# Maxima rows sent between two parts of a packing, and two lone heads scored large, large, small, small

## The chip, the cores and the metric

The kernel runs on one core of a Trainium2 chip. The metric is the time of one execution on the device in microseconds (us); three executions of the kernel before gave 2126.93, 2128.16 and 2131.79, median 2128.16. All profile rows come from one profiled execution of 2130.74 us. Engines: PE is TensorE's matmul, PEld its weight load, DVE is VectorE, ACT is ScalarE, POOL is GpSimd, and SP is SyncE, which here only issues DMAs.

## The reference

Two layers. Layer 0 takes x of shape (2, 2048, 256), normalises it, and runs a differential attention; layer 1 is a small attention over 256 features and a second small attention over its 16 picked heads. The change touches layer 0's attention alone:

```python
q = qkv[..., :2 * Hx].reshape(Bx, 2 * NQ, Sx, HD)        # 32 query heads of 16 features
k = qkv[..., 2 * Hx:2 * Hx + G].reshape(Bx, NKV, Sx, HD) # 8 key heads
scores = jnp.einsum('bhqd,bhkd->bhqk', q, k) / math.sqrt(HD)
scores = jnp.where(causal, scores, -jnp.inf)             # 2048 x 2048, causal
aw = jax.nn.softmax(scores, axis=-1)
aw = aw[:, :, 0] - lam * aw[:, :, 1]
attn = jnp.einsum('bhqk,bhkd->bhqd', aw, v) * (1.0 - LAMBDA_INIT)
```

## The kernel before

Layer 0's attention is done in 16 **groups** (2 batches by 8 key heads); a group has 4 query heads that share one key head. float32 numbers are split into bf16 parts (`part[0]`, `part[1]`, `part[2]`) whose products are added up, so that the PE can multiply in bf16. A product of queries and keys is therefore two matmuls into one bank of PSUM: a **large** one with 64 rows of contraction (four pairs of parts) and a **small** one with 34 rows (two more pairs, and two rows that subtract the query's maximum). The even heads of a group lie in partitions 0 to 63, the odd ones in 64 to 127, so the matmuls of an even and of an odd head use different rows of the PE.

Each group goes over its scores twice. In pass A, 80 **units** find each query's largest score: `unit_head` (L908) makes 128 queries by up to 512 keys for each of two heads, and DVE reduces it (L643, L640). In pass B, 36 **steps** make the softmax: in a step each head's scores of 128 keys by 512 queries are made (`score`, L938), ACT takes the exponential (L771), and the PE multiplies by V two steps later (`meet_v`, L980). Units run ahead of the steps: 46 units of a group are done before its first step, and a table (`PLACES`) says at which places of a step the next units stand. `two_heads(n, hp, u)` scores the two heads of pair `hp` with the unit `u` threaded between them; where the table gives no unit, `u` is None and the two heads stand alone. That is so at six places of each group (step 0 pair 1; steps 2, 3, 10, 20 and 35 pair 0), and in the last group, whose units run out at step 15, at 45 places: 6 x 15 + 45 = 135 in all. At steps 0, 3 and 10 such a matmul has 512 columns, at 2, 20 and 35 it has 256.

The B pass of block j (512 queries; blocks 0 to 3 begin at steps 0, 3, 10 and 21) needs the block's maxima in two rows of `q_pack`. They go from DVE over POOL and the PE to ACT, which copies them to `m_rows` (`take_maxima`, L746); then SP sends them with four small DMAs (`maxima_rows`, L386). The PE waits for these at the block's first step, and the waiting instruction is the large matmul of head 0.

SP also fills the packs of the next group: `pack` issues 36 DMAs of 64 KB (`pack_part`, L314 for keys, L316 for queries; 18 of part 0, 12 of part 1 and 6 of part 2) and one for V (L379). It begins when the last step of the group before is through, which frees the buffers. SP works through its program in order: in iteration g it does the pack of group g + 1, then the maxima rows of block 2 of group g, then the next group's rows to DRAM and back (L351 to L367), then the rows of block 3, and those of blocks 0 and 1 of group g + 1. The PE needs the new pack at the first unit of group g + 1, which stands in step 15.

Of the kernel before, what the change touches and what calls it, by code (L numbers as in the profile page):

```python
# [23 lines left out]
C = 512  # L24
# [18 lines left out]
STEPS = len(B_STEPS)  # L43
# [5 lines left out]
UNITS = len(A_UNITS)  # L49
# [20 lines left out]
def masked(u):  # L70

    return u in MASKED


def width_a(u):
    j, t, c, _ = A_UNITS[u]
    return P * (t + 1) if c == j else C
# [113 lines left out]
def layer0_attention(nc, sems, keep, early, x, Wqkv, lq1, lk1, lq2, lk2, c0, wmod0, c1, wmod1):  # L191
# [3 lines left out]
    with ExitStack() as ctx:  # L195
# [102 lines left out]
        def regions(buf):  # L298

            n = ROWS * 2 * D  # L300
            return scratch[buf][0:n], scratch[buf][n:n + ROWS * P], scratch[buf][n + ROWS * P:]
# [5 lines left out]
        def pack_part(queue, buf, p, sides):  # L307

            for n2 in range(2):
                for r, (pq, pk) in enumerate(zip(PARTS_Q[n2], PARTS_K[n2])):  # L310
                    for side in sides:
                        at = HALF * side + HD * r
                        if pk == p:
                            queue.dma_start(k_pack[buf][at:at + HD, n2, :], part[p][HD * QH:HD * (QH + 1), :]).then_inc(packs_in, 16)  # L314
                        for h in range(side, QH if pq == p else 0, 2):
                            queue.dma_start(q_pack[buf][at:at + HD, h // 2, n2, :], part[p][HD * h:HD * (h + 1), :]).then_inc(packs_in, 16)  # L316
# [5 lines left out]
        @block.sync  # L322
        def _(sp):
            for layer, c in enumerate((c0, c1)):
                for n in range(B):
                    sp.dma_start(cT[:, layer, :, n], c[n, :].rearrange("(k p) -> p k", p=P),
                                 allow_slow_non_contiguous=True).then_inc(cT_in, 16)

            def load_x(n, unused):

                if unused is not None:
                    sp.wait_ge(xhat_ready, upto(unused))
                sp.dma_start(xg[:, :, :], x_rows[bass.ds(upto(n * ROWS), ROWS), :].rearrange("(r p) d -> p r d", p=P)) \
                    .then_inc(x_loaded, 16)

            load_x(0, None)
            sp.dma_start(wmods[:, 0, :, 0:2 * D], wmod0.rearrange("(k p) n -> p k n", p=P)[:, :, 0:2 * D]).then_inc(wmod_a_in, 16)
            sp.dma_start(wqkv[:, :, :], Wqkv.rearrange("(k p) n -> p k n", p=P)).then_inc(wqkv_in, 16)
            load_x(1, 1)
            sp.dma_start(wmods[:, 0, :, 2 * D:6 * D], wmod0.rearrange("(k p) n -> p k n", p=P)[:, :, 2 * D:6 * D]).then_inc(wmod_b_in, 16)  # L340
            sp.dma_start(wmods[:, 1, :, :], wmod1.rearrange("(k p) n -> p k n", p=P)).then_inc(wmod_b_in, 16)
            for k, v in enumerate((lq1, lk1, lq2, lk2)):
                sp.dma_start(lam_in[:, k, :], v.rearrange("(o n) -> o n", o=1).broadcast_to([P, P])).then_inc(lam_inputs, 16)

            def rows_to_dram(n, buf):

                sp.wait_ge(rows_ready, WPARTS * (n + 1))
                q, k, v = regions(buf)  # L350
                sp.dma_start(q.rearrange("(c p r) -> p c r", c=4, p=P), qkvT[:, 0:4, :]).then_inc(rows_out, 16)  # L351
                sp.dma_start(k.rearrange("(p r) -> p r", p=P), qkvT[:, 4, :]).then_inc(rows_out, 16)
                sp.dma_start(v.rearrange("(r p e) -> p r e", r=2, p=P), qkvT[:, 5, :].rearrange("p (r e) -> p r e", r=2)) \
                    .then_inc(rows_out, 16)

            def heads_from_dram(n, buf):


                sp.wait_ge(rows_out, 48 * (n + 1))
                if n:  # L360
                    sp.wait_ge(parts_ready, n)
                q, k, _ = regions(buf)
                by_head = q.rearrange("(b e h r) -> e b h r", b=BLOCKS, e=HD, h=QH)
                for h in range(QH):
                    sp.dma_start(headT[HD * h:HD * (h + 1), :].rearrange("e (b r) -> e b r", b=BLOCKS), by_head[:, :, h, :]) \
                        .then_inc(heads_in, 16)
                sp.dma_start(headT[HD * QH:HD * (QH + 1), :].rearrange("e (a b r) -> e a b r", a=QH, b=BLOCKS // QH),  # L367
                             k.rearrange("(b e a r) -> e a b r", b=BLOCKS // QH, e=HD, a=QH)).then_inc(heads_in, 16)

            def pack(n, buf, steps_done):  # L370

                if steps_done is not None:
                    sp.wait_ge(pv_done, upto(START + steps_done))
                    sp.wait_ge(parts_ready, upto(n + 1))
                for p in range(3):
                    if steps_done is None:
                        sp.wait_ge(*part_made(p))
                    pack_part(sp, buf, p, range(2) if steps_done is not None else (0,))
                sp.dma_start(v_tile[buf][:, :, 0:HD], regions(buf)[2].rearrange("(t p d) -> p t d", p=P, d=HD)).then_inc(v_in[buf], 16)  # L379

            def maxima_rows(count, buf, j):

                sp.wait_ge(m_copied, upto(count))
                for h in range(QH):
                    at = HALF * (h % 2) + SMALL
                    sp.dma_start(q_pack[buf][at:at + 2, h // 2, 1, C * j:C * (j + 1)], m_rows[2 * TB * h:2 * TB * (h + 1), :]) \  # L386
                        .then_inc(m_rows_in, 16)

            rows_to_dram(0, 0)
            heads_from_dram(0, 0)  # L390
            rows_to_dram(1, 1)
            sp.wait_ge(pool_consts, POOL_CONSTS)
            pack(0, 0, None)
            heads_from_dram(1, 1)
            maxima_rows(1, 0, 0)
            maxima_rows(2, 0, 1)

            for g in range(GROUPS):
                par, more = g % 2, g + 2 < GROUPS
                if g == GROUPS - 1:  # L400
                    sp.wait_ge(rows_ready, WPARTS * GROUPS)
                    sp.wait_ge(rows_out, 48 * GROUPS)
                    load_weights(sp)
                if more:
                    load_x(g + 2, g + 2)
                if g + 1 < GROUPS:
                    pack(g + 1, 1 - par, STEPS * g)
                maxima_rows(4 * g + 3, par, 2)
                if more:
                    rows_to_dram(g + 2, par)  # L410
                    heads_from_dram(g + 2, par)
                maxima_rows(4 * g + 4, par, 3)
                if g + 1 < GROUPS:
                    maxima_rows(4 * g + 5, 1 - par, 0)
                    maxima_rows(4 * g + 6, 1 - par, 1)
# [397 lines left out]
        def _(pe):  # L813
# [85 lines left out]
            def unit_head(u, n):  # L899

                j, t, c, hp = A_UNITS[u % UNITS]
                buf, side = u // UNITS % 2, SIDES[n]
                w, q = width_a(u % UNITS), C * j + P * t
                at = 2 * u + n
                rows = slice(HALF * side, HALF * (side + 1))
                if at >= A_RING:
                    pe.wait_ge(a_maxed, at - A_RING + 1)
                ins = pe.matmul(a_bank[at % A_RING][:, 0:w], q_pack[buf][rows, hp, 0, q:q + P], k_pack[buf][rows, 0, C * c:C * c + w],  # L908
                                start=True, stop=not masked(u % UNITS))
                if not masked(u % UNITS):  # L910
                    ins.then_inc(a_scored, 1)
# [32 lines left out]
            def two_heads(n, hp, u):  # L944


                short = u is not None and width_a(u % UNITS) < C
                score(n, 2 * hp, 0)
                if u is not None:
                    unit_head(u, 0)  # L950
                if short:
                    mask_head(u, 0, 0)
                    mask_head(u, 0, 1)
                score(n, 2 * hp, 1)
                if u is not None and not short:
                    mask_head(u, 0, 0)
                    mask_head(u, 0, 1)
                score(n, 2 * hp + 1, 0)
                if u is not None:
                    unit_head(u, 1)  # L960
                score(n, 2 * hp + 1, 1)
                if u is not None:
                    mask_head(u, 1, 0)
                    mask_head(u, 1, 1)

            def meet_v(n):

# [41 lines left out]
            for n in range(TAIL):  # L1009
                g, s = n // STEPS, n % STEPS  # L1010
# [858 lines left out]
```

## Time and profile before

| what | value |
|---|---|
| executions | 2126.93, 2128.16, 2131.79 us |
| profiled execution, its span | 2130.74 us, 2129.2 us |
| PE busy | 2016.2 us (95%) |
| DVE busy | 1731.2 us (81%) |
| ACT busy | 1499.7 us (70%) |
| POOL busy | 689.2 us (32%) |

The span runs from the first to the last instruction; 1.5 us of the execution lie around it. Groups of layer 0 begin at about 103.8 us and repeat every 104 us or so until 1752; layer 1 and what lies between follow. A waits row gives who waited for whom: us in total, times, the longest. A timeline row gives start and length in us, engine, line, operation, tiles, the shape of the first instruction, how many were joined, and in brackets the idle time before the first and what ended it. Instructions of one line are joined even where their shapes differ. A windows row gives a stretch, its length, each engine's busy time and count, the granted clock as a share of 2.4 GHz, and the DMA engines' share and rate.

### The profile page before, as it was taken

Reading aid. Unit: us, or ns where it says so; the run is one execution under the profiler, and the core shown is the slowest. Engines: PE = TensorE matmul, PEld = TensorE weight load, DVE = VectorE, ACT = ScalarE, POOL = GpSimd, SP = SyncE. Lnnn points to the kernel's source line nnn. Section 1 sums busy time; section 2 is a strip of 40 time slices with the busy share of each in tenths; the row PEclk is TensorE's granted clock in tenths of the full one; section 3 lists DMA queues with packets and bytes.
Section 4 is the critical chain, followed back from the end, with each engine's and each line's share of the span. In section 5 each row is a group of like instructions: output and inputs, shape, how many; then the busy total and the mean of one; then the engine's idle time right before and its main releaser. Section 6 shows DMA issues by size and latency. Waiting matters only on the chain. (4 is left out here: it accounts for less than half of the span.)

```text
span 2129.2 us, 43957 instructions
## 1 busy us (share of the span) xinstructions
PE 2016.2 (95%) x16204; PEld 904.0 (42%) x16204; DVE 1731.2 (81%) x3986; ACT 1499.7 (70%) x3065; POOL 689.2 (32%) x1246
## 2 busy tenths in 40 slices
PE   7899999999999999999999999999989999979895
PEld 6243433343334343434333333333333328746674
DVE  3989898989898989898989898888889927833788
ACT  2178787878787878887878878787868782423664
POOL 2214141414232333323232324242411213410678
PEclk8599999999999999999999999999999999989998
DMA  7230403031313122222212121313120003110111
GB/s 179 32 61 8 74 14 69 19 64 24 59 27 55 33 49 39 44 45 38 47 35 49 34 51 31 54 29 54 29 48 23 12 1 99 40 50 1 31 50 50
DMA packets 138423, 93.10 MB, mean 44 GB/s; under 512 B 90977, under 2 KB 127969, under 8 KB 138209
## 3 DMA queue, kind: packets, MB, share of 16 engines
q1 hardware_dynamic: 137632, 89.12, 20.4%
q8 instruction: 128, 2.10, 0.4%
q10 hardware_dynamic: 576, 1.18, 0.3%
q14 instruction: 87, 0.70, 0.1%
HBM read 31.00 MB, written 20.97 MB: 24 GB/s over the span
## 5 line engine op out<-in xcount | busy, mean ns | idle before, releaser
L771 ACT ACTIVATE probs<-b_bank 128x512 f32<-128x512 f32 (+1 forms) x2304 | 1156.6, 579 | 261.8 <-PE b_bank L938 255.0
L643 DVE TENSOR_REDUCE m_part<-a_bank 128x1 f32<-128x512 f32 (+3 forms) x2016 | 1168.8, 636 | 158.5 <-PE a_bank L908 115.7
L938 PE MATMUL b_bank<-q_pack,k_pack 34*128 34x512 bf16 (+7 forms) x5120 | 869.9, 347 | 17.6 <-DMA q_pack<-m_rows 17.6
L908 PE MATMUL a_bank<-k_pack,q_pack 64*128 64x512 bf16 (+3 forms) x2560 | 811.5, 357 | 19.4 <-DVE m_part L643 14.1
L980 PE MATMUL acc<-probs,v_tile 128*32 128x512 f32 (+3 forms) x5120 | 588.3, 541 | 3.1 <-POOL probs L508 0.8
L938 PEld LDWEIGHTS b_bank<-q_pack,k_pack 34*128 34x128 bf16 (+1 forms) x5120 | 309.1, 94 | 456.4 <-ACT probs L771 327.2
L908 PEld LDWEIGHTS a_bank<-k_pack,q_pack 64*128 64x128 bf16 x2560 | 237.4, 94 | 322.7 <-DVE m_part L643 204.9
L508 POOL TENSOR_SCALAR_AFFINE_SELECT probs<-probs 128x512 f32<-128x512 f32 (+1 forms) x192 | 151.7, 790 | 643.3 <-ACT probs L771 643.2
L640 DVE CUSTOM_DVE_ANT_0 a_bank<-a_bank,mask_a 128x384 f32<-128x384 f32 (+3 forms) x544 | 251.6, 513 | 33.3 <-PE a_bank L908 31.8
L980 PEld LDWEIGHTS acc<-probs,v_tile 128*32 128x32 f32 x5120 | 108.1, 108 | 161.3 <-issue 96.7
L523 POOL TENSOR_TENSOR o_w<-o_rl,signs 128x16 f32<-128x16 f32 x64 | 14.4, 226 | 418.7 <-DVE o_rl L666 418.7
L918 PE MATMUL a_bank<-future,pick 64*128 64x128 bf16 x960 | 128.3, 218 | 0.0
L475 POOL TENSOR_TENSOR rest<-headT,part 80x256 f32<-80x256 f32 x120 | 98.1, 818 | 0.0
L918 PEld LDWEIGHTS a_bank<-future,pick 64*128 64x128 bf16 x960 | 83.4, 95 | 22.7 <-issue 1.0
L740 ACT ACTIVATE part<-headT 80x256 bf16<-80x256 f32 x128 | 82.0, 651 | 2.7 <-DMA headT<-scratch 2.7
L480 POOL TENSOR_TENSOR part<-rest,part 80x256 bf16<-80x256 f32 x120 | 80.0, 667 | 9.6
L844 PE MATMUL b_bank<-hT,wqkv 128*128 128x256 f32 x280 | 79.7, 407 | 0.0
L640 DVE DVE_READ_ACCUMULATOR2_ANT m_part<- 128x1 f32 x544 | 76.8, 141 | 0.0
L732 ACT ACTIVATE qkvT<-b_bank 128x256 f32<-128x256 f32 x84 | 32.2, 383 | 58.4 <-PE b_bank L844 44.6
L1499 PE MATMUL score_banks<-qkT 128*128 128x512 f32 (+3 forms) x160 | 66.2, 546 | 0.9 <-DVE attn L1572 0.9
L844 PEld LDWEIGHTS b_bank<-hT,wqkv 128*128 128x128 f32 x280 | 47.8, 190 | 30.2 <-ACT probs L771 19.7
L490 POOL TENSOR_TENSOR m_neg<-zeros,m_max 128x16 bf16<-128x16 f32 x64 | 14.1, 221 | 139.4 <-DVE m_max L650 139.4
(206 smaller groups left out, 1722.0 us busy)
## 6 DMA issues: line engine op xcount, KB each, us to landing
q_pack<-part SPq DMA_DIRECT2D x372, 64.0 KB, 2.4
k_pack<-part SPq DMA_DIRECT2D x186, 64.0 KB, 2.3
headT<-scratch SPq DMA_DIRECT2D x80, 128.0 KB, 3.9
scratch<-qkvT SPq DMA_DIRECT2D x16, 512.0 KB, 2.9
xg<-in_L_attn_x SPq DMA_DIRECT2D x16, 256.0 KB, 2.7
scratch<-qkvT SPq DMA_DIRECT2D x32, 128.0 KB, 2.9
q_pack<-m_rows SPq DMA_DIRECT2D x256, 2.0 KB
x<-in_L_attn_x SPq DMA_DIRECT2D x16, 256.0 KB, 6.2
```

What stands on the lines that cost most here:

```text
L475: pool.tensor_tensor(piece(rest, i, PIECES), by_position(i, PIECES), piece(part[0], i, PIECES), ALU.subtract) \
L480: ins = pool.tensor_tensor(piece(part[2], i, PIECES), piece(rest, i, PIECES), piece(part[1], i, PIECES), ALU.subtract)
L508: pool.affine_select(out=blk, in_=blk, compare_op=ALU.is_ge, fill=0.0, base=0, pattern=[[0, QH]] + [[0, blocks]] * (blocks > 1) + [[1, P]] ...
L640: dve.tensor_tensor_reduce(out=bank[:, 0:w], in0=bank[:, 0:w], in1=mask_a[:, C - w:C], scale=1.0, scalar=NEG, op0=ALU.add, op1=ALU.max, ac ...
L643: dve.tensor_reduce(out, bank[:, 0:w], AX.X, ALU.max).then_inc(a_maxed, 1)
L740: act.activation(piece(part[0], i, PIECES), by_position(i, PIECES), ACT.Copy).then_inc(part0_ready, 1)
L771: act.activation(probs[:, n % P_RING, h, at:C], b_bank[bank_no(("B", n, h))][:, at:C], ACT.Exp, scale=HD ** -0.5) \
L844: ins = pe.matmul(bank[:, 0:D], wqkv[:, k, P * w:P * (w + 1)], hT[:, k, :], start=k == 0, stop=k == 1)
L908: ins = pe.matmul(a_bank[at % A_RING][:, 0:w], q_pack[buf][rows, hp, 0, q:q + P], k_pack[buf][rows, 0, C * c:C * c + w], start=True, stop= ...
L918: ins = pe.matmul(a_bank[at % A_RING][:, w - P:w], pick[rows, m, :], future[rows, m, :], start=False, stop=m == 1)
L938: ins = pe.matmul(b_bank[bank_no(slot)][:, at:at + C - q], k_pack[par][rows, n2, P * kt:P * (kt + 1)], q_pack[par][rows, h // 2, n2, C * j ...
L980: ins = pe.matmul(acc[32 * h:32 * (h + 1), q:C], v_tile[par][:, kt, :], probs[:, n % P_RING, h, at:at + C - q], start=kt == 0, stop=s == J ...
```

## The change

Two edits, which don't depend on each other. First, `pack` can take the arguments of a `maxima_rows` call and makes it after part 0's DMAs; in iteration g the rows of block 2 are sent there and no longer behind the whole pack. The last iteration, which has no pack, sends them as before. Second, `two_heads` without a unit issues large, large, small, small and no longer large, small, large, small. With a unit nothing changes.

```diff
-            def pack(n, buf, steps_done):
+            def pack(n, buf, steps_done, rows=()):
...
                     pack_part(sp, buf, p, range(2) if steps_done is not None else (0,))
+                    if p == 0 and rows:
+                        maxima_rows(*rows)
...
                 if g + 1 < GROUPS:
-                    pack(g + 1, 1 - par, STEPS * g)
-                maxima_rows(4 * g + 3, par, 2)
+                    pack(g + 1, 1 - par, STEPS * g, (4 * g + 3, par, 2))
+                else:
+                    maxima_rows(4 * g + 3, par, 2)
...
             def two_heads(n, hp, u):
-                short = u is not None and width_a(u % UNITS) < C
+                if u is None:
+                    for small in range(2):
+                        for h in range(2 * hp, 2 * hp + 2):
+                            score(n, h, small)
+                    return
+                short = width_a(u % UNITS) < C
```

SP's queue in the first iteration of the loop, kernel before. `part0` to `part2` are the parts, `q_pack0` is the pack that group 0 is being scored from, `k_pack1` and `q_pack1` are those of group 1:

```order
L314 DMA k_pack1<-part0 16x2048 x2
L314 DMA k_pack1<-part1 16x2048 x2
L316 DMA q_pack1<-part1 16x2048 x4
L314 DMA k_pack1<-part1 16x2048
L316 DMA q_pack1<-part1 16x2048 x2
L314 DMA k_pack1<-part1 16x2048
L316 DMA q_pack1<-part1 16x2048 x2
L314 DMA k_pack1<-part2 16x2048 x2
L316 DMA q_pack1<-part2 16x2048 x4
L379 DMA v_tile1<-scratch1 128x16x16
L386 DMA q_pack0<-m_rows 2x4x128 x4
L351 DMA scratch0<-qkvT 128x4x256
```

The same place in the changed kernel (its lines are numbered two or three higher):

```order
L314 DMA k_pack1<-part0 16x2048 x2
L388 DMA q_pack0<-m_rows 2x4x128 x4
L314 DMA k_pack1<-part1 16x2048 x2
L316 DMA q_pack1<-part1 16x2048 x4
L314 DMA k_pack1<-part1 16x2048
L316 DMA q_pack1<-part1 16x2048 x2
L314 DMA k_pack1<-part1 16x2048
L316 DMA q_pack1<-part1 16x2048 x2
L314 DMA k_pack1<-part2 16x2048 x2
L316 DMA q_pack1<-part2 16x2048 x4
L381 DMA v_tile1<-scratch1 128x16x16
L351 DMA scratch0<-qkvT 128x4x256
```

The four maxima DMAs have moved up past 18 pack DMAs and the one of V; nothing else on SP has moved.

The PE at step 10 of group 1, kernel before. The `b_bank` rows are pass B's scores: `b_bank1` is head 0's (large, then small), `b_bank2` head 1's; `a_bank` rows are units:

```order
L908 MATMUL a_bank2<-k_pack1,q_pack1 128x512
L908 MATMUL a_bank0<-k_pack1,q_pack1 128x512
L938 MATMUL b_bank1<-q_pack1,k_pack1 128x512 x2
L938 MATMUL b_bank2<-q_pack1,k_pack1 128x512 x2
L908 MATMUL a_bank1<-k_pack1,q_pack1 128x512
L908 MATMUL a_bank2<-k_pack1,q_pack1 128x512
```

The same place in the changed kernel:

```order
L911 MATMUL a_bank2<-k_pack1,q_pack1 128x512
L911 MATMUL a_bank0<-k_pack1,q_pack1 128x512
L941 MATMUL b_bank1<-q_pack1,k_pack1 128x512
L941 MATMUL b_bank2<-q_pack1,k_pack1 128x512
L941 MATMUL b_bank1<-q_pack1,k_pack1 128x512
L941 MATMUL b_bank2<-q_pack1,k_pack1 128x512
L911 MATMUL a_bank1<-k_pack1,q_pack1 128x512
L911 MATMUL a_bank2<-k_pack1,q_pack1 128x512
```

Head 1's large matmul, with its wait for a free bank, now stands ahead of head 0's small one.

## Rows read from the trace of the kernel before

**Rows 1.** The page's head: the span, and PE's busy time.

```profile
span 2129.2 us, 43957 instructions
...
PE 2016.2 (95%) x16204; PEld 904.0 (42%) x16204; DVE 1731.2 (81%) x3986; ACT 1499.7 (70%) x3065; POOL 689.2 (32%) x1246
```

**Rows 2.** Waits of the whole span: us in total, times, longest.

```profile
PEld b_bank L938 <- DMA q_pack<-m_rows: 21.8, 14, 5.0
...
PE b_bank L938 <- DMA q_pack<-m_rows: 17.6, 13, 4.7
```

**Rows 3.** Timeline of SP in group 1, from the pack's thirteenth issue to the maxima rows.

```profile
218.78 2.48 SPq L316 DMA_DIRECT2D q_pack<-part  x4
221.30 2.48 SPq L314 DMA_DIRECT2D k_pack<-part  x4
...
232.67 2.48 SPq L316 DMA_DIRECT2D q_pack<-part  x4
...
235.82 2.83 SPq L386 DMA_DIRECT2D q_pack<-m_rows  x4
```

**Rows 4.** Timeline of ACT: the copy of block 2's maxima, groups 0 and 1.

```profile
115.14 0.25 ACT L746 ACTIVATE m_rows<-b_bank 32x128 bf16<-32x128 bf16 x1
...
218.19 0.25 ACT L746 ACTIVATE m_rows<-b_bank 32x128 bf16<-32x128 bf16 x1
```

**Rows 5.** Timeline of PE in group 1: step 10's begin, and group 2's first unit.

```profile
238.14 0.39 PE L908 MATMUL a_bank<-k_pack,q_pack 64*128 64x512 bf16 x2
239.73 0.61 PE L938 MATMUL b_bank<-q_pack,k_pack 64*128 64x512 bf16 x4 [1.20 <-DMA q_pack<-m_rows]
...
257.66 0.23 PE L908 MATMUL a_bank<-k_pack,q_pack 64*128 64x128 bf16 x1
```

**Rows 6.** Windows: steps 9 and 10 of groups 0, 14 and 15.

```profile
131.72:139.03 7.31, 7.18 (x61) 3.34 (x62) 5.24 (x9) 3.52 (x9) 1.73 (x2) 1.00 0.00 0
1584.96:1596.90 11.94, 6.92 (x53) 2.13 (x51) 6.20 (x11) 3.36 (x8) 1.73 (x2) 0.86 0.29 42
1687.62:1693.75 6.13, 5.58 (x55) 2.04 (x51) 6.11 (x11) 3.36 (x8) 1.73 (x2) 1.00 0.01 1
```

**Rows 7.** Windows: steps 9 and 10 of groups 1, 3 and 9, sum over groups 1 to 13.

```profile
235.00:243.17 8.17, 6.97 (x61) 3.25 (x62) 5.34 (x9) 3.52 (x9) 1.73 (x2) 1.00 0.28 35
...
442.95:450.26 7.31, 7.10 (x59) 3.35 (x60) 5.24 (x9) 3.52 (x9) 1.73 (x2) 1.00 0.22 24
...
1064.49:1075.13 10.64, 8.55 (x61) 3.84 (x60) 5.33 (x9) 3.52 (x9) 1.73 (x2) 0.84 0.25 34
...
sum 105.55, PE 92.59 PEld 43.13 DVE 69.16 ACT 45.81 POOL 22.53; mean PE 7.12 PEld 3.32 DVE 5.32 ACT 3.52 POOL 1.73
```

**Rows 8.** Windows: step 11 to the next group's step 9, six groups' sum.

```profile
sum 575.77, PE 568.45 PEld 217.01 DVE 516.78 ACT 479.82 POOL 183.66; mean PE 94.74 PEld 36.17 DVE 86.13 ACT 79.97 POOL 30.61
```

**Rows 9.** Windows: from just behind the two longest stalls (groups 9, 14).

```profile
1070.63:1074.04 3.41, 3.41 (x23) 1.54 (x20) 1.29 (x2) 1.09 (x2) 0.00 (x0) 0.50 0.00 0
...
1592.87:1596.28 3.41, 3.25 (x22) 0.88 (x22) 1.29 (x2) 1.08 (x2) 0.00 (x0) 0.50 0.00 0
```

**Rows 10.** The page's DMA issues: the pack's queries, us to landing last.

```profile
q_pack<-part SPq DMA_DIRECT2D x372, 64.0 KB, 2.4
```

**Rows 11.** Timeline of PE in two narrow windows at 239.8 and 240.15 us.

```profile
239.73 0.39 PE L938 MATMUL b_bank<-q_pack,k_pack 64*128 64x512 bf16 x2 [1.20 <-DMA q_pack<-m_rows]
...
239.96 0.38 PE L938 MATMUL b_bank<-q_pack,k_pack 34*128 34x512 bf16 x2
```

**Rows 12.** Timeline of the last group, steps 25 to 27: PE (narrow windows), PEld, ACT.

```profile
1727.96 0.39 PE L938 MATMUL b_bank<-q_pack,k_pack 64*128 64x512 bf16 x2
...
1728.19 0.38 PE L938 MATMUL b_bank<-q_pack,k_pack 34*128 34x512 bf16 x2
...
1728.74 0.11 PEld L938 LDWEIGHTS b_bank<-q_pack,k_pack 64*128 64x128 bf16 x2 [0.24 <-ACT probs L771]
...
1726.63 4.04 ACT L771 ACTIVATE probs<-b_bank 128x512 f32<-128x512 f32 x8 [0.27 <-PE b_bank L938]
1730.92 4.04 ACT L771 ACTIVATE probs<-b_bank 128x512 f32<-128x512 f32 x8 [0.25 <-PE b_bank L938]
```

More of the change, by code:

```diff
@@ L944, in two_heads @@
             def two_heads(n, hp, u):
-                short = u is not None and width_a(u % UNITS) < C
+                if u is None:
[4 more added lines that the diff above has]
+                short = width_a(u % UNITS) < C
                 score(n, 2 * hp, 0)
-                if u is not None:
-                    unit_head(u, 0)
+                unit_head(u, 0)
                 if short:
@@ L954, in two_heads @@
                 score(n, 2 * hp, 1)
-                if u is not None and not short:
+                if not short:
                     mask_head(u, 0, 0)
@@ L958, in two_heads @@
                 score(n, 2 * hp + 1, 0)
-                if u is not None:
-                    unit_head(u, 1)
+                unit_head(u, 1)
                 score(n, 2 * hp + 1, 1)
-                if u is not None:
-                    mask_head(u, 1, 0)
-                    mask_head(u, 1, 1)
+                mask_head(u, 1, 0)
+                mask_head(u, 1, 1)
             def meet_v(n):
```

## The prediction

> **What bounds the kernel now.** I read the page first: PE is busy for 95% of the span [rows 1], so time is saved where the PE stands still or where it issues less. Next the list of waits. Among the PE's own waits in layer 0 the largest is one DMA, the maxima rows: 13 stalls of 17.6 us in all, the longest 4.7 us; its weight loads show a fourteenth, too short for the PE's row [rows 2]. One stall in each of groups 1 to 14 is what this makes. Third, the timeline around one of them. In group 1 the last two unit matmuls start at 238.14, head 0's large one of step 10 could follow 0.22 us later, and starts at 239.73 [rows 5]. SP issued the rows at 235.82 to 238.65, right behind the pack [rows 3], though ACT had copied them at 218.19 [rows 4]. The data was ready 17 us before it was sent: what is late is SP's queue, and nothing else.
>
> Last, windows over the groups. From step 11 to the next group's step 9, six groups (0, 1, 3, 7, 9 and 11) take 575.77 us, 95.96 each [rows 8]; group 0 has no stall ahead of that stretch and group 9 one of the longest. So a stall's price sits wholly in steps 9 and 10 of its group.
>
> **Edit 1, what it removes.** Sent behind the 18 DMAs of part 0, the rows leave SP much earlier. The pack's thirteenth to sixteenth issue start at 218.78; the next row joins four, of which the first two are part 0's last, at 0.62 us each [rows 3]: part 0 is through at 221.30 + 2 x 0.62 = 222.5. The copy at 218.19 is older, so SP doesn't wait. The four issues take 2.83 us and end at 225.4, and what lay between the last issue's end and the PE's start before, 239.73 - 238.65 = 1.08 us, puts the landing at 226.5. The PE asks at 238.36: 11.9 us to spare. The stall goes in all 14 groups.
>
> **What is late next.** The price of a stall is not its length. Where there is no stall (group 0) steps 9 and 10 take 7.31 us [rows 6]; group 3, where the PE idles 0.21 of them, takes 7.31 too; group 1, where it idles 1.20, takes 8.17, that is 0.86 more [rows 7]. Some 0.2 to 0.35 us of each stall only stand where the PE would else wait for DVE to empty a bank, since DVE has 5.3 us of work in these steps either way. So I take windows and not the waits row:
>
> - groups 1 to 13: 105.55 us in sum [rows 7], less 13 x 7.31 = 95.03, gives 10.52 us. It contains group 9 with 10.64 - 7.31 = 3.33 us.
> - group 14: 11.94 us, its twin without a stall is group 15 with the same units and steps and no projections: 6.13 us [rows 6]. That gives 5.81 us.
>
> Sum: 16.3 us. The raw stalls are 17.6; the absorbed part takes some 3 to 4 us off, and the clock puts most of it back. In groups 9 and 14 the granted clock is 0.50, the lower level (1.2 GHz), for 3.41 us from about the end of the two longest stalls [rows 9], while it stays at 1.00 in groups 1 and 3. With the stalls gone the PE is busy there and I expect both drops to go. The difference of windows already contains them. The Trainium skill ("TensorE: Matmul & The Clock Gate", Part 1) says that the default is throttled and activity releases it; the two rows agree, and the shorter stalls without a drop show that the length matters.
>
> **What edit 1 adds.** 18 pack DMAs and V's go out four issues, 2.8 us, later. Before, the last pack issue of group 1 ends at 232.67 + 2.48 = 235.15 [rows 3] and lands 2.4 us later [rows 10]: now at about 240.4, and the PE uses the pack first at 257.66 [rows 5], about 1 us earlier in the new kernel. 16 us remain. In group 0 the copy comes later, at 115.14 [rows 4], so SP stands there with half a pack behind it: 23 issues of 0.63 to 0.7 us from 115.4 end at 130.3, landed by 132.7; the use is at 139.03 + 14.49 = 153.5 (the same distance behind step 11 as 257.66 has behind 243.17). Cost nothing. What comes next on SP (the next group's rows to DRAM) waits for ACT anyway, and the rows' total number of issues is the same.
>
> **Edit 2.** 135 pairs are reordered. Which order does the PE run? In the order before, head 0's small matmul stands between the two large ones and needs the same PE rows as the first; if the PE kept to it, head 1's large one could not start before 239.73 + 0.22. But two large matmuls start at 239.73 and have both ended 0.39 us later, and two small ones follow together at 239.96 [rows 11]; in the last group the same at 1727.96 and 1728.19 [rows 12]. The PE already pairs them: two slots of 0.22 us and not three. I take 0 for the edit. The Trainium skill says the opposite ("TensorE: Matmul & The Clock Gate", Part 3, The mechanism): matmuls are monotone in start and end, strict first in, first out. By that rule each reordered pair would save a slot; this trace doesn't agree, with two starts at 239.73 where the rule allows one, and the measurement decides.
>
> Upper end of the gain, if the rows misled me: a slot of 0.22 us at three places of a group and half of it at three, 0.98 us by 15 groups = 14.7, and in the last group no more than what ACT idles there, 0.27 us in two steps by some ten pairs of steps [rows 12] = 2.7: 17.4 us. Lower end: head 1's large matmul waits for its bank, and head 0's small one now stands behind it. The wait seen is 0.24 us at 1728.74 [rows 12]. If nothing hid it: ten such places in the last group and one in each of 15 others, 25 x 0.24 = 6.0 us lost. I take 0, nearest to what the rows show, because ACT is then still at the exponentials of the step before (eight back to back in 4.04 us [rows 12]) and would not begin head 0's sooner.
>
> **The sum.** The profiled execution: 2130.74 - 16.3 = 2114.4 us. It stands 2.6 us above the median of the three runs, 2128.16. Stretches without a stall repeat closely (7.31 twice, 95.96 as the mean of six), so I think that the runs differ by stalls, and by a clock drop like group 9's: there the PE was busy for 3.41 us at half its clock [rows 9], which costs up to 1.7. From the median, then, 16.3 - 1.7 = 14.6 comes off: 2113.6. Between the two I predict 2114.
>
> **Rivals.**
> - *Matmuls in strict order* (edit 2 saves slots). For: the page named above. Against: rows 11 and 12. Time: 2114 - 17 = 2097. Chance 0.04.
> - *The gain is given back to DVE.* DVE is busy 86.13 of 95.96 us behind the stall [rows 8], and a PE that runs ahead waits for its banks. Against: groups 0 and 3, with hardly a stall, are in the six whose mean is 95.96. If half goes: 2122. Chance 0.06.
> - *The reorder costs.* Small matmuls queue behind a bank wait, all unhidden: 2114 + 6 = 2120. Chance 0.04.
> - *Slower than before.* SP now waits for ACT's copy in the middle of the pack; if that came late, the second half of the pack would reach the PE late at step 15. It decides from a copy 16 us later than 218.19, and each us beyond costs one in 15 groups; 2 us beyond make 30 us less the 16 gained: 2142. Rows 4 speak against it, the copy follows from work that the change doesn't touch. Chance 0.02.
> - *No effect:* the rows wait elsewhere, for instance behind part 0's 64 KB transfers in the rings, until 11.9 us are used up. A pack DMA lands after 2.4 us [rows 10]. 2128. Chance 0.02.
>
> **The numbers.** The forecast has 0.82. Its own range is 2111 to 2118, since the last part of the program and the runs before scatter by some 2 us. With the neighbours it is 2109 to 2120, which leaves out the 2097 and most of the 2122. A change of 0.2%, 4.3 us, is about what can be told from none. Faster by more than that: forecast and the first three rivals, 0.95. Within: 0.03. Slower: 0.02.
>
> **What would show it.** The wait of L938 on the maxima rows is gone from both lists; SP issues them between pack DMAs, about 12 us after the pack's begin; steps 9 and 10 take 7.3 us in all of groups 1 to 13 and 6.1 in group 14; the clock stays at full through the groups; step 11 to step 9 stays at 95.96. If that last number falls by about 0.7 to 1 us, the PE had run in order after all, and edit 2 has a gain of its own; if it grows, DVE takes back what was won. The forecast is wrong if the wait stays in any group, or if the last group's steps 16 to 35 grow.

## The result and the profile after

| what | before | after |
|---|---|---|
| median, us | 2127.55 (4 runs, 2125.2 to 2131.79) | 2113.17 (4 runs, 2111.92 to 2114.65) |
| ratio | 1 | 0.9931, 95% interval 0.9913 to 0.9948 |
| span of the profiled execution, us | 2129.2 | 2110.8 |

The change is faster by 0.7%, 14.4 us between the medians; each kernel's executions lie within 7 us of each other, and the two sets don't overlap. 2114 was predicted, with 2109 to 2120 as the range.

SP in group 1, changed kernel, timeline; it answers [rows 3]. In the changed kernel L388 stands for the L386 of before, L941 for L938 and L911 for L908; L314 and L316 are where they were.

```profile
217.60 2.49 SPq L316 DMA_DIRECT2D q_pack<-part  x4
220.13 1.22 SPq L314 DMA_DIRECT2D k_pack<-part  x2
221.39 2.66 SPq L388 DMA_DIRECT2D q_pack<-m_rows  x4
224.09 1.19 SPq L314 DMA_DIRECT2D k_pack<-part  x2
...
234.31 2.49 SPq L316 DMA_DIRECT2D q_pack<-part  x4
```

The rows now leave between 221.39 and 224.05, right behind part 0 and with no pause. The PE's timeline in the same group answers [rows 5], first as joined rows, then in two narrow windows:

```profile
236.97 0.39 PE L911 MATMUL a_bank<-k_pack,q_pack 64*128 64x512 bf16 x2
237.20 0.60 PE L941 MATMUL b_bank<-q_pack,k_pack 64*128 64x512 bf16 x4
237.63 0.90 PE L911 MATMUL a_bank<-k_pack,q_pack 64*128 64x512 bf16 x2
...
255.62 0.23 PE L911 MATMUL a_bank<-k_pack,q_pack 64*128 64x128 bf16 x1
```

```profile
237.20 0.38 PE L941 MATMUL b_bank<-q_pack,k_pack 64*128 64x512 bf16 x2
...
237.41 0.38 PE L941 MATMUL b_bank<-q_pack,k_pack 34*128 34x512 bf16 x2
```

The row of the kernel before that belongs beside the 0.90 us, the two units behind its step 10, and the page's group of L941, which tells of the changed kernel's whole span:

```profile
240.18 0.38 PE L908 MATMUL a_bank<-k_pack,q_pack 64*128 64x512 bf16 x2
```

```profile
L941 PE MATMUL b_bank<-q_pack,k_pack 34*128 34x512 bf16 (+7 forms) x5120 | 869.2, 347 | 0.1
```

Step 10 follows the units after 0.23 us with nothing in brackets. L938 waited 17.6 us for the rows [rows 2]; the last number of L941's row is its idle time from any cause, 0.1 us. But the two units behind step 10 now take 0.90 us and no longer 0.38: the second stands until DVE has emptied a bank. Before, DVE did that during the stall. This is the absorbed part, seen at its place.

Windows of the changed kernel: steps 9 and 10 of groups 0, 14 and 15, beside [rows 6], then their sum over groups 1 to 13, beside [rows 7]; last the sum of the same six stretches from step 11 to step 9, beside [rows 8].

```profile
130.56:137.87 7.31, 7.18 (x59) 3.35 (x60) 5.24 (x9) 3.53 (x9) 1.74 (x2) 1.00 0.17 17
1573.15:1579.28 6.13, 5.59 (x55) 2.03 (x51) 6.11 (x11) 3.36 (x8) 1.74 (x2) 1.00 0.48 84
1670.00:1676.13 6.13, 5.58 (x55) 2.03 (x51) 6.11 (x11) 3.36 (x8) 1.74 (x2) 1.00 0.01 1
...
sum 94.97, PE 93.22 PEld 43.45 DVE 68.12 ACT 45.84 POOL 22.62; mean PE 7.17 PEld 3.34 DVE 5.24 ACT 3.53 POOL 1.74
...
sum 575.76, PE 568.41 PEld 216.43 DVE 516.93 ACT 480.07 POOL 184.21; mean PE 94.73 PEld 36.07 DVE 86.16 ACT 80.01 POOL 30.70
```

105.55 - 94.97 = 10.6 and 11.94 - 6.13 = 5.8 us: 16.4 in all. The rest is where it was, 575.76 against 575.77. The spans differ by 18.4; the other 2.0 us lie ahead of group 0's first step (1.1) and behind step 10 of the last group (0.8), where the rows of edit 1 play no part. The kernel with edit 1 alone, below, reaches step 9 of group 0 2.0 us later than this one (132.56 against 130.56), so such amounts are scatter between executions. The medians differ by 14.4 and the windows by 16.4: the two are taken from different executions, and the kernel before moves by some us from one to the next.

### The profile page after: what moved, and what is told of

Its sections match the earlier page's. It is cut to its first block and busy times, and to the rows that moved or that the text cites. A ratio compares the mean times of both kernels' runs of the same rounds, so it can differ in the third digit from the quotient of the medians.

```text
span 2110.8 us, 43957 instructions
## 1 busy us (share of the span) xinstructions
PE 2012.3 (95%) x16204; PEld 900.5 (43%) x16204; DVE 1730.5 (82%) x3986; ACT 1500.6 (71%) x3065; POOL 691.0 (33%) x1246
## 5 line engine op out<-in xcount | busy, mean ns | idle before, releaser
L646 DVE TENSOR_REDUCE m_part<-a_bank 128x1 f32<-128x512 f32 (+3 forms) x2016 | 1167.9, 637 | 145.4 <-PE a_bank L911 103.0
L941 PE MATMUL b_bank<-q_pack,k_pack 34*128 34x512 bf16 (+7 forms) x5120 | 869.2, 347 | 0.1
L911 PE MATMUL a_bank<-k_pack,q_pack 64*128 64x512 bf16 (+3 forms) x2560 | 814.9, 356 | 22.3 <-DVE m_part L646 14.6
L941 PEld LDWEIGHTS b_bank<-q_pack,k_pack 34*128 34x128 bf16 (+1 forms) x5120 | 307.7, 94 | 438.7 <-ACT probs L774 330.2
L911 PEld LDWEIGHTS a_bank<-k_pack,q_pack 64*128 64x128 bf16 x2560 | 238.3, 94 | 330.6 <-DVE m_part L646 213.6
L643 DVE CUSTOM_DVE_ANT_0 a_bank<-a_bank,mask_a 128x384 f32<-128x384 f32 (+3 forms) x544 | 251.8, 513 | 30.7 <-PE a_bank L911 29.2
L921 PE MATMUL a_bank<-future,pick 64*128 64x128 bf16 x960 | 128.3, 218 | 0.0
L921 PEld LDWEIGHTS a_bank<-future,pick 64*128 64x128 bf16 x960 | 83.4, 95 | 22.8 <-issue 1.0
L643 DVE DVE_READ_ACCUMULATOR2_ANT m_part<- 128x1 f32 x544 | 77.3, 142 | 0.0
```

The lines of the kernel that those rows point to most:

```text
L643: dve.tensor_tensor_reduce(out=bank[:, 0:w], in0=bank[:, 0:w], in1=mask_a[:, C - w:C], scale=1.0, scalar=NEG, op0=ALU.add, op1=ALU.max, ac ...
L646: dve.tensor_reduce(out, bank[:, 0:w], AX.X, ALU.max).then_inc(a_maxed, 1)
L921: ins = pe.matmul(a_bank[at % A_RING][:, w - P:w], pick[rows, m, :], future[rows, m, :], start=False, stop=m == 1)
L941: ins = pe.matmul(b_bank[bank_no(slot)][:, at:at + C - q], k_pack[par][rows, n2, P * kt:P * (kt + 1)], q_pack[par][rows, h // 2, n2, C * j ...
```

## The experiments

The kernel before was run again beside each set: medians 2127.29 (17 runs; edit 1 alone, edit 2 alone, group 14, head by head), 2131.34 (9 runs; behind part 2, behind part 1, ahead of the pack, small 0 ahead) and 2126.98 (13 runs; the two swaps in one pair). Ratios are against those. The changed kernel was not run again: "over the changed kernel" always means over 2113.17, and since the kernel before moved by 4 us between the sets, such a difference of one or two us says nothing.

**Edit 1 alone.** `two_heads` as before, `pack` as changed. Against the changed kernel, the last line in words:

```diff
-                if u is None:
-                    for small in range(2):
-                        for h in range(2 * hp, 2 * hp + 2):
-                            score(n, h, small)
-                    return
+                (the large, small, large, small order of the kernel before)
```

> Edit 1 alone: block 2's maxima rows behind part 0's DMAs, the two lone heads large, small, large, small as before. My theory (the whole gain is edit 1's, the PE pairs the heads in either order): 16 to 18 us under the kernel before, ratio 0.992, and in steps 9 and 10 7.31 us in groups 1 to 13 and 6.13 in group 14. Rival (the reorder has a share of its own, some 0.7 to 1 us a group, hidden in the sum): 2 to 10 us slower than the changed kernel, step 11 to step 9 at 95.96 here.

Measured: 2113.49 us, ratio 0.9928 (0.9915 to 0.9941): 13.8 us faster, which is the gain of the whole change, though less than the 16 to 18 that were expected from the windows. In its profile the sum over groups 1 to 13 and that of the six stretches are:

```profile
sum 95.00, PE 93.26 PEld 43.48 DVE 68.11 ACT 45.81 POOL 22.53; mean PE 7.17 PEld 3.34 DVE 5.24 ACT 3.52 POOL 1.73
...
sum 575.69, PE 568.40 PEld 216.94 DVE 516.62 ACT 479.80 POOL 183.68; mean PE 94.73 PEld 36.16 DVE 86.10 ACT 79.97 POOL 30.61
```

**Edit 2 alone.** `two_heads` as changed, the maxima rows behind the pack.

> Edit 2 alone: two lone heads large, large, small, small, the maxima rows still behind the whole pack. My theory: within 0.1% of the kernel before, stalls on the maxima rows of 17 us or so as before, step 11 to step 9 at 95.96. Rival (PE in strict order, each lone pair saves a slot of 0.22 or 0.11 us): 10 to 17 us faster. Rival (small matmuls behind a bank wait): up to 6 us slower.

Measured: 2129.9 us (12 runs), ratio 1.0005 (0.9993 to 1.0016): nothing, with 0.16% as the interval's upper end. Its waits, its group 14 and its six stretches:

```profile
PEld b_bank L938 <- DMA q_pack<-m_rows: 17.8, 12, 5.5
...
PE b_bank L938 <- DMA q_pack<-m_rows: 14.3, 12, 5.2
```

```profile
1577.69:1590.69 13.00, 7.46 (x53) 2.34 (x51) 6.52 (x12) 3.44 (x9) 1.73 (x2) 0.75 0.30 45
...
sum 575.70, PE 568.41 PEld 216.30 DVE 516.69 ACT 479.82 POOL 183.71; mean PE 94.74 PEld 36.05 DVE 86.11 ACT 79.97 POOL 30.62
```

The stalls are there, and the stretches hold five of a group's six reordered pairs with no difference over 0.1 us in 576. The two runs together settle the split: edit 1 brings all of the gain that can be seen, and edit 2 nothing that its interval (1.5 us faster to 3.4 slower) and the stretches would show.

**The rows of group 14 alone behind the pack again.**

```diff
-                    pack(g + 1, 1 - par, STEPS * g, (4 * g + 3, par, 2))
-                else:
+                    pack(g + 1, 1 - par, STEPS * g, (4 * g + 3, par, 2) if g != GROUPS - 2 else ())
+                if g >= GROUPS - 2:
                     maxima_rows(4 * g + 3, par, 2)
```

> The changed kernel with the maxima rows of group 14 alone sent behind the pack again. My theory (price of that stall 5.8 us, of which about 1 us is the drop of the granted clock behind it): 5.0 to 6.0 us slower than the changed kernel, steps 9 and 10 of group 14 at 11.1 to 12.1 us, granted clock 0.50 for some 3.4 us behind the stall. Rival (the drops at 1070 and 1593 us were chance and not the stalls' doing): 4.8 us slower, clock at full.

Measured: 2119.03 us, ratio 0.9956 (0.9941 to 0.997), 5.9 us over the changed kernel. Its windows, group 14's steps 9 and 10 and then the part of them at the lower clock:

```profile
1573.16:1585.95 12.79, 7.45 (x54) 2.35 (x51) 6.50 (x11) 3.42 (x9) 1.73 (x2) 0.73 0.29 43
1579.09:1585.92 6.83, 4.35 (x28) 1.50 (x30) 1.74 (x3) 1.11 (x3) 0.00 (x0) 0.50 0.10 10
```

```profile
PE b_bank L941 <- DMA q_pack<-m_rows: 5.0, 1, 5.0
```

One stall of 5.0 us costs 12.79 - 6.13 = 6.66 here, so 1.66 more than its length, and the granted clock stands at 0.50 around its end. The drop was expected for 3.4 us and lasted 6.83, and the window came out above the 11.1 to 12.1 expected. Only 4.35 of the 6.83 us have the PE at work: the clock fell while the PE still stood, and at half the clock 4.35 us of work lose up to 2.2, by estimate. The clock drop belongs to the stall and isn't chance: in this kernel it is the only one in groups 1 to 15, and the changed kernel has none there.

**The rows behind part 2, ahead of V's DMA** (`if p == 2 and rows` for `p == 0`).

> The maxima rows of block 2 behind all 36 pack DMAs but ahead of V's one: one issue, 0.63 us, earlier than in the kernel before. My theory (a stall costs its delay less 0.5 us in groups 1 to 13, nothing under that; its full length in group 14): 3.2 us of 10.5 stay in groups 1 to 13 and some 5 of 5.8 in group 14, so 7 to 10 us slower than the changed kernel and 5 to 9 faster than the one before. Rival (price is the raw stall): 14 x 0.63 = 8.8 us faster than before at least.

Measured: 2121.28 us, ratio 0.9949 (0.9936 to 0.9963), 8.1 us over the changed kernel and 10.1 under the one before. Steps 9 and 10 of group 14, and of groups 1 to 13 in sum:

```profile
1577.22:1588.30 11.08, 6.89 (x55) 2.13 (x53) 6.21 (x11) 3.36 (x8) 1.73 (x2) 0.85 0.33 48
```

```profile
sum 97.44, PE 92.41 PEld 43.11 DVE 68.52 ACT 45.84 POOL 22.54; mean PE 7.11 PEld 3.32 DVE 5.27 ACT 3.53 POOL 1.73
```

97.44 - 95.0 = 2.4 us for 3.2 expected, and 11.08 - 6.13 = 4.95 for 5. Its waits list:

```profile
PE b_bank L941 <- DMA q_pack<-m_rows: 8.1, 7, 3.9
```

The longest, 3.9 us, is group 14's. If the others cost their length, groups 1 to 13 would take 13 x 7.31 + 8.1 - 3.9 = 99.2 us, and they take 97.4. The total alone doesn't tell the rival off: it asked for at least 8.8 us under the kernel before, and 10.1 came.

The price can be read stall by stall. Over groups 1 to 13 of the three kernels that have stalls there (the one before, edit 2 alone, this one), the six stalls of up to 0.30 us leave steps 9 and 10 at 7.31 us. The 25 of 0.36 to 1.63 us lengthen them by the stall less 0.34 us, each within 0.01; the row of 1.20 [rows 5] and its 8.17 [rows 7] are one of them. Only the one of 2.09 us, group 9's before, costs more than its length, 3.33; 1.6 of that are then the clock drop's. So 0.34 us of a stall are absorbed here, not the half microsecond that was expected.

**The rows behind part 1** (`if p == 1 and rows`).

> The rows behind parts 0 and 1, 12 issues or 7.6 us later than in the changed kernel. It had 11.9 us to spare in groups 1 to 13, and in group 14 some 9.4 (the PE asks there at about 1588.2, its rows would be in at 1578.8). My theory: no change, within 0.1% of the changed kernel, no stall on the rows. Rival (part of what was gained is used up by rows that come closer): a few us slower.

Measured: 2113.41 us, ratio 0.9913 (0.99 to 0.9927) and 0.2 us over the changed kernel; no wait on the rows in its lists, and 95.00 us in groups 1 to 13. The rows leave at 228.94 in group 1, 8.1 us later than in the changed kernel if the group's own shift is taken off; behind part 2 they leave at 235.43, 12.4 later.

**The rows ahead of the whole pack.**

```diff
+                if rows:
+                    maxima_rows(*rows)
                 for p in range(3):
                     ...
-                    if p == 0 and rows:
-                        maxima_rows(*rows)
```

> The rows ahead of the whole pack, so that SP stands with all 37 DMAs behind it until ACT has copied the maxima, 7.6 us after the pack could begin. By the changed kernel's spare time at step 15 (16 us) the pack is still in time: no change, within 0.1% of the changed kernel. Rival (the pack is late at step 15, or crowds the rows sent to DRAM for the next group): a stall on pack DMAs before group g + 1's first unit, 1 us or more a group, 15 us or more in all.

Measured: 2113.24 us, ratio 0.9916 (0.9902 to 0.9929), 0.1 us over the changed kernel. SP in group 1:

```profile
218.29 2.58 SPq L388 DMA_DIRECT2D q_pack<-m_rows  x4
220.91 0.58 SPq L314 DMA_DIRECT2D k_pack<-part  x1
...
243.27 2.48 SPq L316 DMA_DIRECT2D q_pack<-part  x4
```

The pack's last four DMAs leave nearly 9 us later than in the changed kernel (243.27 against 234.31; 0.9 of it is the group's own shift) and still the PE doesn't wait for them. Three places for the rows, 0, 18 and 30 pack issues deep, give the same time; behind part 2, 36 deep, they are too late.

**Head by head in the pairs that have a unit.** Edit 2 gained nothing because the PE seemed to start matmuls out of their order. If that were all, order would be free elsewhere too. A pair with a unit is issued large 0, unit 0, small 0, large 1, unit 1, small 1; unit 0 uses the rows of head 1's matmuls, unit 1 those of head 0's. The masks of a unit now follow directly behind it.

```diff
                 score(n, 2 * hp, 0)
-                unit_head(u, 0)
                 ...
                 score(n, 2 * hp, 1)
+                unit_head(u, 0)
                 ...
                 score(n, 2 * hp + 1, 0)
-                unit_head(u, 1)
                 score(n, 2 * hp + 1, 1)
+                unit_head(u, 1)
```

> The changed kernel, but the pairs that do have a unit are issued in the worst order for a PE that keeps to it: head 0 large, small, then the unit's matmul on the other rows, then head 1 large, small, then the unit's second. Strict order would need four slots where there are three now, 0.1 to 0.22 us more at each of some 1000 pairs: 100 to 200 us slower than the changed kernel. My theory (a matmul whose rows are free starts ahead of older ones that wait for other rows): within 1%, at most a few us either way from the masks' and waits' places.

Measured: 2192.12 us, ratio 1.0297 (1.0283 to 1.0312), 79 us over the changed kernel. Both expectations miss, and strict order with its 100 to 200 us by less than mine, so it had to be looked at again. My first reading was that the unit's second matmul, which waits for a bank, now stood last and alone.

**Only small 0 ahead of unit 0.**

```diff
                 score(n, 2 * hp, 0)
+                score(n, 2 * hp, 1)
                 unit_head(u, 0)
                 ...
-                score(n, 2 * hp, 1)
```

> The changed kernel; in a pair with a unit, head 0's small matmul goes ahead of the unit's first one and nothing else moves, so the unit's second matmul, which waits for DVE, keeps its place ahead of head 1's small one. If the PE kept strictly to its order this would need a fourth slot (0.1 to 0.22 us at each of about 1000 pairs, 100 to 200 us). My theory (a matmul whose rows are free starts ahead of older ones on other rows, and what cost the head-by-head order 79 us was the waiting matmul standing last and alone): within 0.3% of the changed kernel.

Measured: 2198.43 us, ratio 1.0312 (1.0298 to 1.0326), 85 us over. So that reading fell: unit 1 kept its place here and the loss is larger. The traces tell what it is. In this kernel PE, in two narrow windows, and DVE (starts are measured, the ends of matmuls are modelled by the profile):

```profile
730.59 0.39 PE L941 MATMUL b_bank<-q_pack,k_pack 64*128 64x512 bf16 x1
730.59 0.39 PE L911 MATMUL a_bank<-k_pack,q_pack 64*128 64x512 bf16 x1
...
730.81 0.38 PE L941 MATMUL b_bank<-q_pack,k_pack 34*128 34x512 bf16 x2
...
731.26 0.69 DVE L646 TENSOR_REDUCE m_part<-a_bank 128x1 f32<-128x512 f32 x1 [0.26 <-PE a_bank L911]
```

The unit's matmul starts together with large 0 although small 0 stands between them: there are still three slots, the third at 731.03, and not the four of a strict order. It ends at 730.98. DVE waits for it and starts at 731.26, 0.28 later, and 0.07 behind the end of small 0 at 731.19. In the changed kernel, at a place where DVE waits for a unit that is in front of the small one:

```profile
703.54 0.39 PE L941 MATMUL b_bank<-q_pack,k_pack 64*128 64x512 bf16 x1
703.54 0.39 PE L911 MATMUL a_bank<-k_pack,q_pack 64*128 64x512 bf16 x1
```

```profile
703.97 0.69 DVE L646 TENSOR_REDUCE m_part<-a_bank 128x1 f32<-128x512 f32 x1 [0.20 <-PE a_bank L911]
```

703.93 to 703.97: 0.04 us. From the unit's start, which is measured, DVE begins 0.43 us later here and 0.67 in the other kernel. Over all waits of DVE of more than 0.05 us (410 and 576) the median distance from the last unit's end is 0.042 us in the changed kernel and 0.282 here, where the distance from the last small matmul's end is 0.072 with nine tenths of them at or under 0.089.

The trace also records each update of a semaphore, and that needs no modelled end. In the swapped kernel small 0's signal goes out at 731.205 and the unit's, which had started 0.22 us ahead of it, at 731.239; in the changed kernel the unit's goes out at 703.948, 0.02 behind its end. Of the 2000 or so unmasked units of a run, none in the changed kernel signals more than 0.2 us behind its end. With the swap 707 do, each 0.034 or 0.035 us behind a small matmul's signal. Starts go by free rows; the signal of completion goes out in program order.

**The swap in pair 0 alone, and in pair 1 alone** (the diff above under `if hp == 0`, and under `if hp == 1`). If late signals are the cause, the loss must sit in the pair whose unit DVE is waiting for. In the waits above that is pair 1; at pair 0 DVE has older banks to work on.

> The swap of the run before (head 0's small matmul ahead of the unit's first), in pair 0 alone. My theory now (a matmul starts as soon as its rows are free, ahead of older ones on other rows, but its completion is signalled in program order, so the unit's signal waits for the small matmul in front of it, 0.22 us): it costs only where DVE stands waiting for that unit, and at pair 0 DVE still has older banks to reduce. At most 15 us slower than the changed kernel. Strict order of starts: half of the 85 us that the swap cost in both pairs, some 40.

> The swap in pair 1 alone, where DVE was seen idle until the unit's signal. My theory (late signal): nearly all of the 85 us, 65 to 85 slower than the changed kernel. Strict order of starts: some 40.

Measured: pair 0 2123.27 us, ratio 0.9979 (0.997 to 0.9989), 10 us over the changed kernel; pair 1 2194.5 us, ratio 1.0315 (1.0298 to 1.0332), 81 us over. Order of starts was expected to cost some 40 us in either. By the semaphores' updates the late signals are about as many in the two, 338 and 369; what differs is whether DVE waits. DVE's waits for units in the waits lists, changed kernel, then pair 0, then pair 1 (L646 reduces plain units behind L911 and masked ones behind L921, L643 masked ones on its own):

```profile
DVE m_part L646 <- PE a_bank L911: 103.0, 193, 0.9
DVE m_part L646 <- PE a_bank L921: 34.3, 102, 0.6
DVE a_bank L643 <- PE a_bank L911: 29.2, 44, 1.1
```

```profile
DVE m_part L646 <- PE a_bank L911: 106.2, 193, 0.9
DVE m_part L646 <- PE a_bank L921: 34.5, 109, 0.6
DVE a_bank L643 <- PE a_bank L911: 32.0, 44, 1.1
```

```profile
DVE m_part L646 <- PE a_bank L911: 143.1, 255, 1.2
DVE a_bank L643 <- PE a_bank L911: 56.7, 107, 1.3
DVE m_part L646 <- PE a_bank L921: 46.3, 117, 0.7
```

The three sums are 166.5, 172.7 and 246.1 us. DVE's added wait is 79.6 us of the 81 with the swap in pair 1, and 6.2 of the 10 in pair 0.

## Why the prediction was right, point by point

- *The stalls go, since SP's queue was all that was late.* Right; edit 1 alone brings the whole gain, and putting one group's rows back brings that stall back. The spare time of 11.9 us holds too: rows that leave 8.1 us later are free, 12.4 us later (behind part 2) they aren't.
- *The price is the difference of windows, 10.5 + 5.8 us, not the 17.6 us of waits.* Right to 0.1 us: 10.6 + 5.8. Had I taken the waits the result would have been near as well, but by luck: about 4.4 us absorbed and 3.2 us of clock drops have opposite signs (estimates from the prices above). The kernel behind part 2 separates them, with 2.4 us in groups 1 to 13 where the raw stalls are 4.2. The 0.2 to 0.35 us that each stall was said to absorb are 0.34.
- *Both clock drops go.* Right. That the stall causes them was argued from two rows and is now shown for group 14; for group 9's no run brings that stall back. The size is not steady: a stall of 5.0 us had 6.83 us at the lower clock around its end, one of 4.7 us had 3.41 [rows 9].
- *The pack's later half costs nothing.* Right. Its last DMAs leave 2.8 us later against the group's begin, as worked out (234.31 against 232.67, and the group begins 1.17 us earlier), and there is more room than was used: with the rows ahead of the pack it is free too.
- *Edit 2 is worth 0.* Right, measured alone at 1.0005. Its reason, that the PE already paired the heads, holds in the traces, since neither a pair's starts (two large ones at 237.20, two small ones 0.21 us later, as at 239.73 and 239.96 before [rows 11]) nor the stretches moved. The lower bound, 6 us lost behind bank waits, never showed: from step 16's begin to step 35's the last group takes 41.35 us in both kernels.
- *Edit 2's reason was only half of the mechanism.* It said nothing of when a completion is signalled. In a lone pair the large matmuls carry no signal that anyone waits for, so signals in program order cost nothing there. With a unit in the pair someone does, and moving one small matmul costs 85 us.
- *The time.* 2114 for 2113.17. That the hit is as close as 0.8 us is partly luck: the base was a choice between 2114.4 and 2113.6, while the median of the kernel before moved by 4 us between sets. The reason given for the base, that runs differ by their stalls, is made likely and not shown: the kernels with early rows and no swap spread over 2 to 4 us in 4 or 5 runs, and pair 0's swap over 4.0 in 10, while the kernel before spreads over 6 to 9 in 9 to 17 runs and edit 2 alone over 10.6 in 12. But behind part 2, with seven stalls left, the spread is 2.0 in 5. The chances given to the forecast and the first three rivals add to 0.96, not 0.95.

## What to carry to other kernels

A few small DMAs that the compute waits for soon, queued behind many that it needs much later, are late for no other reason than their place; the data's time of readiness against its time of issue shows it at once. Price a stall by the length of the same steps where it is absent, because a neighbouring engine catches up in it and a long one can drop the clock. And on the PE, ask of each matmul who waits for its completion, and put nothing that ends later in front of it. In these runs the PE itself sorted out the order in which matmuls of different rows start.

## What the runs showed of the hardware

- Matmuls on disjoint rows of the PE start out of program order: a pair issued large, small, large, small starts both large ones within 0.01 us (at 239.73 [rows 11]), as one issued large, large, small, small does (at 237.20), and the small ones 0.22 us later. The Trainium skill ("TensorE: Matmul & The Clock Gate", Part 3, The mechanism) has starts and ends in program order; of the starts this case's runs show otherwise.
- Completion is signalled in program order: with one older small matmul in front, the unit's signal went out at 731.239, 0.034 us behind the older one's and 0.26 behind its own end, and DVE started 0.28 us behind that end (medians of 576 waits: 0.28, and 0.04 without the swap). The Trainium skill has, in the same section, the last-issued matmul finish last; the order of the signals agrees, and of the ends the trace has only modelled times.
- Signals about 0.24 us late, for one unit of two in a step, cost 81 us over the kernel where DVE was waiting for them (369 late ones among unmasked units), and 10 where it mostly was not (338).
- Of the PE's stalls on the maxima rows, the one of 3.9 us (behind part 2) and the one of 4.7 us (before) had 3.41 us at 1.2 GHz around or behind their end, and those of 5.0 us (group 14's rows) and 5.2 us (edit 2 alone) had 6.83. One of 2.1 us (group 9, before) had 3.41 too. All those of up to 1.6 us left the clock at 2.4 GHz.
- In steps 9 and 10 a stall of the PE costs its length less 0.34 us if it lasts 0.36 to 1.63 us (25 stalls), and nothing up to 0.30 us (six stalls): during it DVE empties a bank for which the PE would else have waited.
